# Splitting the weighing of gathered units between two engines in the preparation stage

## The reference, cut to what matters

```python
xproj = inp @ in_w + in_b
x1 = depthwise 3x3 convolution(x) + dw_b;  x1 = gelu(layer_norm(x1))
offset = x1 @ off_w + off_b
mask = softmax((x1 @ mask_w + mask_b).reshape(N, H, W, G, P), -1)
# per pixel, group (G = 16) and tap (P = 9): four corners of xproj, weighed bilinearly and by the mask
samp = (v00 * (1 - wx) + v01 * wx) * (1 - wy) + (v10 * (1 - wx) + v11 * wx) * wy
out = einsum('hwpc,hwp->hwc', samp, m) @ out_w + out_b
```

## Time and profile before

| | |
|---|---|
| runs | 14348.79, 14355.92, 14365.49 us; median 14355.92 |
| profiled execution | 14375.56 us, of which the span is 14373.9 us |
| mean granted TensorE clock | 0.771 |
| busy, share of the span | PE 59%, DVE 68%, ACT 34%, POOL 66% |

### The profile page before, as it was taken

How to read it: one execution, slowest core, us unless ns; L and a number is a source line. 1 busy time by engine, 2 the same in 40 slices (tenths; PEclk the granted TensorE clock), 3 DMA queues, 4 the chain that set the end, 5 groups by cost and what they waited for, 6 DMA issues and landing times. The chain is left out here.

```text
span 14373.9 us, 109977 instructions
## 1 busy us (share of the span) xinstructions
PE 8550.2 (59%) x32544; PEld 4159.5 (29%) x32544; DVE 9751.2 (68%) x9864; ACT 4857.6 (34%) x13537; POOL 9445.4 (66%) x9221
## 2 busy tenths in 40 slices
PE   6773657356664558446664558446664558555667
PEld 3241324122332324222332224222332324222223
DVE  6755976569764886569765886569765986544443
ACT  3232533145321543145321543145322543122221
POOL 0005777777777777777777777777777777777771
PEclk7886778667887679767887679767887679777778
DMA  1011111321133111421133111421133112432221
GB/s 69 9 31 58 52 58 56 102 78 52 58 84 105 52 50 58 110 79 52 58 83 104 52 56 52 113 76 52 58 83 105 52 59 60 106 111 94 72 78 48
DMA packets 905628, 1001.99 MB, mean 70 GB/s; under 512 B 697681, under 2 KB 707921, under 8 KB 893074
## 3 DMA queue, kind: packets, MB, share of 16 engines
q0 software_dynamic: 294912, 604.57, 14.9%
q1 hardware_dynamic: 610066, 389.88, 8.8%
HBM read 814.38 MB, written 179.39 MB: 69 GB/s over the span
## 5 line engine op out<-in xcount | busy, mean ns | idle before, releaser
L133 POOL DMA_INDIRECT gat<-corner_tables,idx x9216 | 9445.0, 1025 | 4626.3 <-issue 2484.6
L170 DVE TENSOR_REDUCE dcn<-gat 128x32 f32<-128x1152 f32 x1024 | 2161.7, 2111 | 320.0 <-ACT gat L150 287.2
L150 ACT ACTIVATE gat<-gat,wts 128x32 f32<-128x32 f32 x8752 | 1906.9, 306 | 962.1 <-DMA gat<-corner_tables,idx 961.2
L164 DVE TENSOR_TENSOR gat<-gat,wts 128x1152 f32<-128x1152 f32 (+3 forms) x1024 | 1094.5, 1069 | 1672.9 <-DMA gat<-corner_tables,idx 1559.7
L797 PE MATMUL PS<-hc,ident 128*128 128x512 f32 (+2 forms) x4096 | 1963.9, 639 | 233.9 <-DVE hc L841 192.6
L864 DVE TENSOR_TENSOR_SCAN hs<-dA,PS 128x1024 f32<-128x1024 f32 x672 | 1531.9, 2280 | 45.5 <-ACT dA L814 18.1
L797 PEld LDWEIGHTS PS<-hc,ident 128*128 128x128 f32 x4096 | 1018.4, 281 | 858.7 <-issue 477.5
L1152 ACT ACTIVATE E<-PS,nmax 128x1024 f32<-128x1024 f32 x512 | 570.5, 1114 | 945.2 <-DVE nmax L1209 774.0
L1073 PE MATMUL PS<-ident,E 128*128 128x128 f32 x4096 | 600.9, 294 | 427.7 <-ACT ET L1142 226.9
L841 DVE TENSOR_TENSOR hc<-hs,PS 128x1024 f32<-128x1024 f32 x672 | 802.0, 1193 | 0.8 <-issue 0.8
L1742 PE MATMUL PS<-late_M,wp 128*32 128x512 f32 x4480 | 632.3, 715 | 267.0 <-DVE wp L1783 184.6
(11 more groups left out here) (251 smaller groups left out, 11481.2 us busy)
## 6 DMA issues: line engine op xcount, KB each, us to landing
gat<-corner_tables,idx POOLq DMA_INDIRECT x9216
corner_tables<-xp SPq DMA_DIRECT2D x1024, 64.0 KB, 2.2
D<-in_dist_dram SPq DMA_DIRECT2D x8, 4096.0 KB, 13.8
keep_scratch<-X SPq DMA_DIRECT2D x15, 2048.0 KB, 11.3
weighted<-M SPq DMA_DIRECT2D x56, 512.0 KB, 2.8
late_M<-weighted SPq DMA_DIRECT2D x7, 4096.0 KB
wqkv<-in_qkv_w_dram SPq DMA_DIRECT2D x8, 3072.0 KB, 11.5
X<-keep_scratch SPq DMA_DIRECT2D x12, 2048.0 KB, 15.9
```

What stands on the lines that cost most here:

```text
L133: nc.gpsimd.indirect_dma_start(bd.gat[n % self.NG][:, k * 4 * CG:(k + 1) * 4 * CG], None, bd.rows, bass.IndirectOffsetOnAxis(ap=bd.idx[:, ...
L150: ins = nc.scalar.activation(block, block, ACT.Copy, scale=weights[:, i:i + 1])
L164: nc.vector.tensor_tensor(v, v, wv, ALU.mult).then_inc(self.prod, 1)
L170: nc.vector.tensor_reduce(bd.dcn[m % 2][:, g * CG:(g + 1) * CG], gat[:].rearrange("p (k c) -> p c k", c=CG), AX.X, ALU.add).then_inc(self. ...
```

## The change

The preparation is given `blocks=16`. DVE multiplies 20 of the 36 blocks of each unit there, and ScalarE the other 16 by six calls of `scale` in its program, which ask for the units up to 4, 9, 10, 13, 23 and 26 of 26 of the stage.

```diff
-            self.background(block, self.share["prepare"], first=store)
+            self.background(block, self.share["prepare"], first=store, blocks=16)
...
                     nc.scalar.activation(xp[m % 4][:], PS[:, m % 4, :], ACT.Copy).then_inc(xp_ready, 1)
                 for t in range(CT):
+                    if t % 2 == 0:
+                        self.scale(act, 4 + 5 * (t // 2), 26)
                     act.wait_ge(dw_sum, t + 1)
                     nc.scalar.activation(x1[:, t, :].rearrange("p (a f) -> p a f", a=2),
                                          PS[:, 4 + 2 * (t % 2):6 + 2 * (t % 2), :], ACT.Copy).then_inc(dw_ready, 1)
+                self.scale(act, 10, 26)
                 for t in range(CT):
                     act.wait_ge(cent, t + 1)
...
                 nc.scalar.activation(rs[:], sd[:], ACT.Exp, scale=-0.5).then_inc(sd_ready, 1)
+                self.scale(act, 13, 26)
                 for t in range(CT):
                     act.wait_ge(normed, t + 1)
                     nc.scalar.activation(x1[:, t, :], x1[:, t, :], ACT.Gelu, scale=self.col("ln_g", t),
                                          bias=self.col("ln_b", t)).then_inc(gelu_out, 1)
+                self.scale(act, 23, 26)
                 act.wait_ge(e_in, 1)
                 e = tmp[:, 0:PT * NMSK]
                 nc.scalar.activation(e, e, ACT.Exp).then_inc(e_out, 1)
+                self.scale(act, 26, 26)
```

## The result

The kernel is slower: 14454.9 us median of 4 runs (14437.5 to 14480.3) against 14352.4 (14342.8 to 14365.5), ratio 1.0076 with a 95% interval of 1.0063 to 1.0089. That is 109 us (90 to 128), where 14,510 was forecast, +153: the right direction and inside the range, but 44 us too much, or 1.4 times what was measured. The profiled execution took 14480.3 us, 25 above its median, around a span of 14478.7.

What follows compares the result with a forecast made beforehand. POOL was taken to set each image's period. Six images at 23 us plus 15 for image 1 give +153 us on the 14355.9 median: 14,509, say 14,510; range 14,440 to 14,595.

Steps and rivals of the forecast that it cites:

- The bound: Whole span: POOL's gather rows set each image's period, 1600 of 1609 us; time POOL loses comes back nowhere.
- The place: Preparation: `scale(4)` stands behind all eight evictions, but DVE needs u0 at its second call; 23 us lost an image.
- First stall: Preparation of image 7: POOL's u5 waits for u0's late scaling and reduction; 20.6 us.
- ScalarE's blocks: ScalarE's multiplies in the preparation: 16 overlapping blocks take 3.5 us a unit; 4.9 if not overlapped.
- Relief: POOL's rows beside DVE's multiply, shorter by 0.54 us: 0.5 us a unit taken off the delay.
- Images 2 to 6 ... I take them as image 7: Preparations of images 2 to 6: same program and share as image 7, so 23 us each.
- second stall: Preparation: POOL's u11 waits for u6, scaled only behind `rs`; 22.0 us late in all.
- Rival 1: POOL relieved by DVE's shorter multiply, 61 us over 114 units: 14,295; needs u0 scaled before 12262; chance 0.04.
- Rival 2: DVE's waits for landings, some 170 us an image, take up the delay; time stays at 14,356; chance 0.04.
- Rival 3: DVE's whole delay reaches the end, through blocks at 4.9 us or 34 us at normalising: 14,587; chance 0.14.
- Rival 4: Table stores run faster with POOL quiet, eighth eviction up to 2.5 us sooner: 100 us, 14,456; chance 0.18.

Runs made afterwards that it cites:

- The wait by itself: Against the kernel before: no unit split; DVE holds each preparation's first reduction until ScalarE's eighth eviction of `xp` is out; ratio 1.0088, 126 us slower.
- the run without ScalarE: Against the kernel before: DVE multiplies 20 of 36 blocks in the preparations, ScalarE none, 16 summed without their weight; ratio 0.9961, 56 us faster.
- the repeat: The unaltered change, run again on another chip against the kernel before; ratio 1.0082.
- placed: Against the kernel before: ScalarE multiplies 16 blocks of each split unit soon after landing, before DVE wants it; 105 units split; ratio 0.9964, 52 us faster.

## Why the prediction was right or wrong

- **The bound.** Right. POOL's waits went up, its rows down, and the time followed. On the page DVE is busy 64 us less (9687.7 against 9751.2) and ScalarE 389 more (5246.8 against 4857.6), and neither shows in the total.
- **The place.** Right, and step by step, image 7, less 86.04: u0 reduced at 12284.2 (forecast 12284.5), u5's first row at 12284.45 (12284.8), centring 12342.2 (12342.8), u6 reduced 12362.3 (12363.0), normalising 12365.6 (12366.5), u11's first row 12362.55 (12363.1). First stall 20.3 for 20.6, 21.5 behind the second for 22.0. The wait by itself, 126 us, shows this as the cause.
- **ScalarE's blocks** at 3.5 us for 16. Right: 3.48 to 3.50 in the rows shown. The estimate of 5.2 from the Trainium skill ("ScalarE: Activation LUTs", "Rules for kernel authors") adds sixteen activations up as if each ran alone. One by itself does take nearly that budget here, 0.306 us, but behind one another they start every 0.21, as the row decided. No table load was added either: the group of each line that has them is as large as before, 8 at each of the four of this stage.
- **Relief**: the step that was mis-sized. "From u11 to u15 I add 1.5 for the normalising ... and take off 5 x 0.5" gave -1.0. The last unit landed 18.9 us late (12522.06 less 86.04, against 12417.10), so it was -2.6. Counted by what DVE does beside each of POOL's rows in this stretch, those beside the multiply lost 1.8 us (0.36 a unit), those beside the normalising gained 1.0, and 1.7 went for which I had no term: POOL, shifted against DVE, no longer meets two operations of the position arithmetic (L1443 and L1474). So 0.5 a unit was about right, as in the run without ScalarE (0.46 to 0.47), and it is the other operations of DVE that I left out. From u5 to u11 too the relief was larger than I had it: POOL was ready for u11 at 12355.0, not 12359, but the wait for u6 swallowed that. The list came 20.8 us late in image 7, not 23.
- **"Images 2 to 6 ... I take them as image 7"** held, but for 3 us. From first tap to list the change added 17.9, 17.4, 21.6, 22.5, 21.8 and 20.8 us in images 2 to 7, 122 in all where I had 138; image 1 added 15.7 for my 15. Of the 16 us that are missing, 13 are six times the 2.2 of image 7. Sum 138 for 153, and 129 when repeated, with 15.3 for image 1 and 17.7 to 20.1 for the others. The images fall into two kinds by the second stall: POOL waits 5.2 us for it in images 2 and 3, and 7.5 to 8.2 in the others. In the repeat only image 3 has 7.5 us, and it is the one with 20.1; the others wait 5.2 to 6.0. Why u6 comes later in some preparations than in others was not tried.
- **The rest**, from 138 or 129 in the stage to 109 or 117 in the total, lies outside the preparations, mainly in the seven stretches between them, whose sum differs from profile to profile by up to 59 us (9721 to 9780). I had no term for that.
- **Rival 1** had its size: the whole relief was priced at 61 us, and without stalls it is 56 (alone) and 52 (placed). It fell on what it was said to need, u0 scaled in time. The rule of the Trainium skill ("SBUF — State Buffer", "Who interferes with whom") that a DVE instruction with two SBUF inputs contends with a GpSimd instruction that reads SBUF agrees with POOL's rows becoming shorter, by 0.46 to 0.47 us a unit, as the multiply becomes shorter by 0.54.
- **Rival 2** (taken up elsewhere) fell by the same runs. **Rival 3** (all 34 us of DVE's delay at the end) fell: normalising was 32.8 us late, the list 20.8. **Rival 4** said that the table stores would run faster with POOL quiet, and the eighth eviction come up to 2.5 us sooner. It starts 59.5 us after the first tap (12364.02 against 12304.56), where it was 59.8, and in the other images it moves by -0.5 to +1.1: its mechanism is refuted. That its time, 14,456, lies 1 us from the measured one is luck.

## What to carry to other kernels

When work is handed to an idle engine, look at what stands ahead of it in that engine's queue and at when its consumer wants the first piece: idle time is of use only between those two. Here the same 16 blocks cost 117 us behind eight evictions that wait for stores, and gain 52 a few lines higher, each behind the eviction that follows its landing. A count of blocks is a poor price: half the blocks kept four fifths of the loss. And an engine that is on no critical path can be worth relieving if its instructions stretch those of the one that is, as DVE's multiply did POOL's rows (2.11 us where 0.95 is normal), which shows in the second engine's row times and not in any wait.

## What the runs showed that was not expected

- A multiply shorter by 0.54 us made POOL's rows in the preparations shorter by 0.46 to 0.47 us a unit when ScalarE had no part (1036.6 us against 1089.0 and 1090.7), but by 0.63 to 0.66 in the change (1015.9 in both profiles, 114 units) and with the placed blocks (1022.8, 105 units). There, as in image 7 above, nearly all of POOL's rows also miss the two operations that are L1443 and L1474 in the kernel before. Going on from 20 to 12 blocks on DVE (0.82 to 0.55 us) brought nothing that the times can tell.
- The stretches outside the preparation differ by up to 59 us between executions of kernels whose programs are the same there, while the preparations of two executions of the kernel before sum to 1484.6 and 1484.7.
